# Transformer layer on one Trainium2 core: queries and keys by seven block products instead of eight, ahead of the attention loop

## What is computed

```
h = layernorm(x) * (1 + ca) + sa               # ca, sa, ga, ... are rows of silu(c) @ wmod, per batch
q = h @ Wq + bq ; k = h @ Wk + bk ; v = h @ Wv + bv          # (4, 512, 16 * 128)
w = softmax(q k^T / sqrt(128) + causal mask)   # per batch and head
x = x + ga * ((w v) @ Wo + bo)
h = layernorm(x) * (1 + cb) + sb
x = x + gb * (top-2 of 8 experts, SwiGLU, + a shared SwiGLU)(h)
```

## Time and profile before

| | us |
|---|---|
| three runs | 1672.33, 1673.3 (median), 1673.81 |
| the profiled execution's own time | 1676.7 |
| its span, first to last instruction | 1674.9 |
| TensorE busy (share) | 1591.5 (95%) |
| VectorE, ScalarE, GpSimd busy (share) | 891.5 (53%), 697.0 (42%), 591.2 (35%) |
| mean granted TensorE clock, share of full | 0.981 |

### The profile page before, as it was taken

The page is one execution under the profiler, slowest core; times in us unless marked ns, Lnnn a source line. Parts: engine busy times, 40 slices in busy tenths (PEclk is TensorE's granted clock), DMA queues, the critical chain, the costliest instruction groups (busy, mean ns, idle before and its releaser), DMA issues.

```text
span 1674.9 us, 29946 instructions
## 1 busy us (share of the span) xinstructions
PE 1591.5 (95%) x9012; PEld 1382.1 (83%) x9013; DVE 891.5 (53%) x2091; ACT 697.0 (42%) x1689; POOL 591.2 (35%) x625
## 2 busy tenths in 40 slices
PE   6999989999999999999999999978998899999997
PEld 3888578888888888888888888767898798888886
DVE  4333136666666566656665666767656322222267
ACT  4222155555555555555555555432231232222332
POOL 0001024544554535444545455655211211111043
PEclk9999999999999999999999999989998999999998
DMA  7522225243343253432423442585213445655455
GB/s 262 200 101 106 95 72 164 64 123 116 111 122 103 72 153 96 129 109 78 152 72 107 118 125 66 164 318 193 88 38 132 151 182 182 252 205 192 178 182 176
DMA packets 178453, 232.40 MB, mean 139 GB/s; under 512 B 78600, under 2 KB 137352, under 8 KB 175328
## 3 DMA queue, kind: packets, MB, share of 16 engines
q1 hardware_dynamic: 168112, 204.74, 37.0%
q0 software_dynamic: 5680, 18.62, 3.9%
q10 hardware_dynamic: 4608, 8.39, 1.6%
HBM read 151.70 MB, written 80.00 MB: 138 GB/s over the span
## 4 chain that ended last, share of the span: by engine, by line
PE 79%; DVE 8%; DMA 6%; ACT 3%; issue 3%; SPq 1%; another core or an unknown queue 0%; POOL 0%; ACTq 0%; DVEq 0%; POOLq 0%
PE bank L1118 48%; PE bank L1195 9%; PE bank L1279 7%; PE bank L1230 7%; DMA slot_results<-y_sb 5%; PE bank L1262 4%; PE bank L1131 1%; PE bank L1336 1%; PE bank L1362 1%; DVE o_lo L1604 1%; DVE pt_lo L1602 1%; ACT prob L939 1%; DVE ht_lo L1778 1%; DMA q_transposed<-q_out 1%; ACT o_hi L972 1%
## 5 line engine op out<-in xcount | busy, mean ns | idle before, releaser
L1118 PE MATMUL bank<-w,xt_hi 128*128 (+2 forms) x1136 | 287.0, 335 | 9.9 <-issue 8.2
L939 ACT ACTIVATE prob<-bank,neg_max 128x128 f32<-128x128 f32 (+3 forms) x256 | 134.0, 526 | 241.3 <-DVE neg_max L1643 238.7
L1118 PEld LDWEIGHTS bank<-w,xt_hi 128*128 128x128 f32 x1136 | 198.7, 191 | 22.0 <-issue 15.5
L680 POOL CAST q_hi<-q_raw 128x512 fp32r<-128x512 f32 x64 | 71.2, 1112 | 386.2 <-PE bank L1230 238.2
L1118 PE MATMUL bank<-w,xt_lo 128*128 (+2 forms) x568 | 185.6, 327 | 0.0
L1118 PE MATMUL bank<-w,ht_hi 128*128 (+3 forms) x426 | 142.6, 416 | 19.2 <-DVE ht_lo L1778 19.2
L1778 DVE TENSOR_TENSOR ht_lo<-bank,ht_hi 128x128 fp32r<-128x128 f32 (+1 forms) x213 | 48.4, 283 | 195.8 <-ACT ht_hi L1052 192.0
L1118 PE MATMUL bank<-wv_hi,h_lo 128*128 128x256 f32 x512 | 144.7, 283 | 0.0
L1118 PE MATMUL bank<-wv_lo,h_hi 128*128 128x256 f32 x512 | 144.5, 282 | 0.0
L1118 PE MATMUL bank<-wv_hi,h_hi 128*128 128x256 f32 x512 | 144.3, 282 | 0.0
L951 ACT ACTIVATE prob<-prob,row_inv 128x128 f32<-128x128 f32 (+3 forms) x256 | 136.2, 556 | 1.4
(11 more groups left out here) (203 smaller groups left out, 4081.6 us busy)
## 6 DMA issues: line engine op xcount, KB each, us to landing
ch_raw<-wexp SPq DMA_DIRECT2D x128, 170.0 KB, 2.6
experts_hi<-ch_hi SPq DMA_DIRECT2D x128, 170.0 KB, 2.0
experts_lo<-ch_lo SPq DMA_DIRECT2D x128, 170.0 KB, 2.1
w<-experts_hi SPq DMA_DIRECT2D x10, 2176.0 KB, 8.4
w<-experts_lo SPq DMA_DIRECT2D x10, 2176.0 KB, 15.0
q_transposed<-q_out SPq DMA_DIRECT2D x64, 256.0 KB, 2.0
q_raw<-q_transposed SPq DMA_DIRECT2D x32, 512.0 KB, 4.2
slot_results<-y_sb SPq DMA_DIRECT2D x39, 256.0 KB
```

Source lines behind the costliest of these rows:

```text
L680: pool.tensor_copy(hi, raw).then_inc(split_hi, 1)
L939: ins = act.activation(prob[:, h, ROW_AT[r]:ROW_AT[r] + (r + 1) * P], bank[2 + i % 2][:, at:at + (r + 1) * P], ACT.Exp, bias=neg_max[:, h, ...
L1118: ins = pe.matmul(dst, a, m, start=(k == 0), stop=(k == last))
```

## The change

Stage 1 now makes both queries and keys, all but the queries of the first two pairs by a scheme with seven block products in place of eight. A *unit* is a pair of heads of q or k, a *half* (`half(v)`) is a unit for two batches, taken as a 2 x 2 block matrix product: weights in blocks (two chunks of features) x (head), hidden state in blocks (batch) x (two chunks). 14 units, 28 halves. Each of the seven products is 2 chunks x 3 passes = 6 matmuls of 512 columns in a bank of its own, and the banks are taken in rotation over all eight. Four of the products take sums of weight blocks (made by GpSimd, `sums`), four take sums of blocks of the hidden state (`t_sums`). VectorE combines the seven banks to the four results in seven instructions; ScalarE copies the first bank out. Results of q are stored as before. Results of k are split there (hi on ScalarE, lo on VectorE once and GpSimd three times a half, through a ring of three buffers of 4 KB a partition) and stored to DRAM, 512 KB per result; the loop loads 1 MB of keys a step.

In the loop, the keys' products and their splitting are gone (and the splitting of wk on GpSimd), the probabilities have a buffer per head, and the orders of the queues are rearranged. At the end, the second `c_seed_of` on GpSimd comes after `c_pre(2)` instead of ahead of it.

The new tables and the head of TensorE's order:

```diff
+UNITS = [("q", 2), ("q", 3), ("k", 0), ("q", 4), ("k", 1), ("q", 5), ("k", 2), ("q", 6), ("k", 3), ("q", 7),
+         ("k", 4), ("k", 5), ("k", 6), ("k", 7)]
+HALVES = [(i, s) for i in range(NU - 2) for s in range(2)] + [(NU - 2, 0), (NU - 1, 0), (NU - 2, 1), (NU - 1, 1)]
+PREPARE = {1: 1, **{2 * i: i + 1 for i in range(1, NU - 1)}}
+MOD_AFTER = {4: 2, 8: 4, 12: 5}
+def stage1_order(plain, half):
+    plain(0)
+    plain(1)
+    half(0)
+    plain(2)
+    plain(3)
+    for v in range(1, NV):
+        half(v)
```

TensorE, stage 1 (`plain(b)`: q of the first two pairs for batch b, 48 matmuls; transposes of batch b+1 between):

```diff
+            def plain(b):
+                pe.wait_ge(hlo_ok, b * TT + TT)
...
+            def half(v):
...
+                def product(j, ws, ms):
+                    if free[j]:
+                        pe.wait_ge(*free[j])
+                    q = 0
+                    for (a_hi, a_lo), (m_hi, m_lo) in zip(ws, ms):
+                        for a, m in ((a_hi, m_hi), (a_hi, m_lo), (a_lo, m_hi)):
+                            ins = pe.matmul(bank[to[j]][:, :], a, m, start=q == 0, stop=q == 5)
...
+                product(0, plain_w(0, 0), rows(0))
+                product(1, sum_w(1), t_rows(2))
+                product(2, sum_w(2), t_rows(3))
+                product(3, sum_w(0), t_rows(1))
+                if v == 0:
+                    transposes(2, 0)
+                    transposes(2, 1)
+                product(4, plain_w(2, 0), rows(2))
+                if v == 0:
+                    transposes(2, 2)
+                    transposes(2, 3)
+                product(5, sum_w(3), rows(DC + 2))
+                product(6, plain_w(2, 1), t_rows(4))
```

VectorE and ScalarE, one half:

```diff
+                dve.tensor_tensor(g_s, p6, e1_s, ALU.add).then_inc(half_ok, 1)
+                dve.tensor_tensor(w_s, p7, g_s, ALU.add).then_inc(half_ok, 1)
+                if v in PREPARE:
+                    unit_low(PREPARE[v])
+                dve.tensor_tensor(u_s, p5, g_s, ALU.add).then_inc(half_ok, 1)
+                total(d22, p5, bb, w_s)
+                if v in PREPARE:
+                    sums_low(PREPARE[v])
+                total(d11, p2, ba, e1_s)
+                if kind == "k":
+                    dve.tensor_tensor(ring[n % 3][:, 1, :], g_s, ring[n % 3][:, 0, :].bitcast(F32),
+                                      ALU.subtract).then_inc(k22_ok, 1)
+                total(d12, p3, ba, u_s)
+                total(d21, p4, bb, w_s)
...
+                act.activation(e1_s, bank[half_banks(v)[0]][:, :], ACT.Copy).then_inc(e1_ok, 1)
+                if v in PREPARE:
+                    unit_high(PREPARE[v])
+                if kind == "k":
+                    for k, (done, src) in enumerate(((C22, g_s), (C11, e1_s), (C12, ct[0]), (C21, ct[1]))):
+                        n = 4 * K_NO[v] + k
+                        if n >= 3:
+                            act.wait_ge(k_st[n % 3], 16 * (n // 3))
...
+                        act.activation(ring[n % 3][:, 0, :], src, ACT.Copy).then_inc(kh_ok, 1)
```

A step of the loop on TensorE (before: see the lines above):

```diff
+                    values(0)
+                    values(1)
+                scores(2, n, here)
+                project(0)
+                project(1)
+                scores(3, n, here)
+                project(2)
+                scores(4, n, here)
+                project(3)
+                scores(5, n, here)
+                turn(0)
+                    values(2)
+                    values(3)
+                turn(1)
+                    scores(0, n + 1, there)
+                weigh(0)
+                    scores(1, n + 1, there)
+                weigh(1)
```

(the two queues are given here as lists; in the code they are calls in this order). In the first step ScalarE has `normalise(5); bias_rows(2); bias_rows(3)` ahead of `pt_part(1, 0)`, each `bias_rows` a copy of 128 x 2048. SP loads 1 MB of keys a step ahead (`load_k`). GpSimd: `split_q(1)` goes between the second and third weight chunk, `wk` is gone, and in the tail:

```diff
+                if tail == 1:
+                    c_seed_of(0)
+                if tail >= 0:
+                    c_pre(tail)
                 if last:
                     c_seed_of(1)
-                if tail >= 0:
-                    c_pre(tail)
```

More of the change, by code:

```diff
@@ L1591, in _ @@
-            with dve.Fori(1, B) as b:
-                batch(b)
-            for m in range(2, 6):
-                mod_piece(m)
+                h_low(0, i)
+            stats(1)
+            stats(2)
+            normalise(1)
+            hidden(1, 0)
+            hidden(1, 2)
+            for i in range(TT):
+                h_low(1, i)
+            t_sums(0)
+            unit_low(0)
+            sums_low(0)
+            t_low(0, (2, 3, 4))
+            normalise(2)
+            dve.wait_ge(const_ld, 5 * 16)
@@ L1597, in _, with plain @@
+            def plain(b):
+                if b == 2:
+                    hidden(3, 0)
+                    hidden(3, 2)
+                    for i in range(TT):
+                        h_low(3, i)
+                    t_sums(1)
+                    t_low(1, (2, 3, 4))
+                if b % 2:
+                    t_low(b // 2, (1,))
+            stage1_order(plain, half)
             stage1_over(dve)
```

1072 lines of the change are left out of this document (641 added, 431 removed).

## The result

The changed kernel took 1687.5 us (median of 4 runs, 1685.0 to 1689.2) against 1673.6 us of the kernel before on the same chip: ratio 1.0075, 95% interval 1.0058 to 1.0092. It is slower by 0.6 to 0.9%, where 0.9% faster was forecast. The profiled execution has a span of 1687.4 us, 12.5 more than before.

What follows compares the result with a forecast made beforehand. TensorE, busy 95% of the span, was taken as the bound. Handover +142.0, loop -141.4, tail -17.4 and seed +2.5 sum to -14.3 us, taken off the 1673.3 median: 1659.0 us, range 1637 to 1682.

Steps and rivals of the forecast that it cites:

- Part 1, the count: Matmuls for queries and keys: 1536 before, 1368 after; 168 fewer at 0.227 us each, 38.1 us.
- Part 2, stage 1: Query and key products start at 27.0 us and end at 365.8, with 7.0 us of new TensorE waits.
- the cover that I named: Key halves in stage 1: slow bank reads paid off by q halves in between, so lag costed at nothing.
- the third rival: Stage 1 key halves bound by splitting: 1678 us, chance 0.13; sign: waits on the stores of keys.
- Handover: Between stage 1 and loop: scores start at 377.2 us, first projection at 405.2, which is 142.0 later than before.
- the bare step: First attention step, run without projections: 28 us from the scores' start to the first projection.
- Part 3: Loop step: period falls from 27.375 to 22.5 us, 141.4 us back over 29 steps; keys' loads and GpSimd hidden.
- the wait of 0.9: Each loop step: TensorE idles 0.9 us ahead of `project(0)`, released by VectorE's `o_lo`.
- Part 4: Tail, step 30's projection to last output tile: 52.2 us instead of 69.6, 17.4 less.
- The second seed: Tail, GpSimd: seed after `c_pre(2)`, which waits for `xr`; costs 2.5 us, bounds 0 and 6.
- The one on the other side: Rival in the loop: longer chain, `o_part(1)` late on ScalarE, period from 23.0; at 23.3 1682 us; chance 0.17.
- TensorE stays the bound in the loop: Rival in the loop: period 21.7 us, total 1636 us, chance 0.17.

Runs made afterwards that it cites:

- 10: Changed kernel with the attention loop's two first loads issued behind the first store of the last half: 1692.8 us, ratio 1.0104 to the kernel before.
- 13: Kernel 9 plus 34 matmuls whose result nobody reads, ahead of the first scores: 1645.4 us, ratio 0.9822 to the kernel before.
- 9: Changed kernel with the three loop orders of 7 and both seeds put back as in 3: 1647.5 us, ratio 0.9852 to the kernel before.
- 6: Changed kernel with the next queries' load issued ahead of the next keys' load in every step: 1679.1 us, ratio 1.0028 to the kernel before.
- 7: Changed kernel with the orders of 5 and 6, and the value weights' split behind the third chunk: 1651.9 us, ratio 0.9863 to the kernel before.
- 5: Changed kernel with ScalarE's evacuation of head 1's output ahead of normalise(0) of the next step: 1691.3 us, ratio 1.0124 to the kernel before.
- 1: Changed kernel with the first seed put back behind the first expert chunk of step 30: 1684.6 us, ratio 1.0078 to the kernel before.
- 2: Kernel before with only the first seed moved late, behind all four expert chunks of step 30: 1683.7 us, ratio 1.0073 to the kernel before.
- 3: Changed kernel with both seeds of the last pair put back to their earlier places on GpSimd: 1682.4 us, ratio 1.0035 to the kernel before.
- 12: Kernel 9 plus reordered tail norm work and row-tile loads, with the first row tile's transposes behind the last output tiles: 1645.5 us, ratio 0.9829.
- 8: Changed kernel with the orders of 5 and 6, the value weights' split left behind the fourth chunk: 1657.0 us, ratio 0.9897 to the kernel before.

## Why the prediction was wrong

**Part 1, the count: right.** TensorE's busy time fell by 40.5 us for 38.1.

**Part 2, stage 1: right to the microsecond or so.** Products end at 366.7 (365.8), new waits 6.2 (7.0), and TensorE busy 268.00 of 268.00 us beside the key halves: the cover that I named held, and the third rival fell. Its sign did show, 36.2 us in 16 waits of ScalarE for the stores of keys, and TensorE felt none of it before the handover. The rule behind that rival shows elsewhere. Six instructions of the norm with both inputs in SBUF took 7.4 us (1105.5 to 1112.9) in the last stretch of the changed kernel, with GpSimd busy beside them; 6 x 0.75 are 4.5. The Trainium skill (SBUF — State Buffer, "Who interferes with whom") states that such an instruction contends with GpSimd's reads of SBUF, and the trace agrees, with 0.83 to 1.75 us for each of the six. `v_lo` and TensorE's wait of 4.98 us for it stand behind them, on the tail's path, where I had not looked for it.

**Handover: the landing of a store was mis-sized.** I took 3.2 us for 512 KB from a median of 2.0 for 256 KB; the median of all 64 such stores was 3.0, but with 1.5 MB of loads in front the one that mattered took 7.3, and the scores came at 381.6 for 377.2. The figure fits a store with nothing in front; what I left out was the queue. 10 took the loads away, and the wait for the buffer fell from 5.9 to 2.3 us. The other 2.0 us lie in the bare step (30.0 for 28.0); with TensorE kept busy in the gap (13) it was 28.3 for the 29.2 of 9, so some 0.9 of it can be the clock. The rest stays open.

**Part 3: the period was right, its cover was not.** 22.2 to 22.6 with 0.6 to 1.2 idle is what most ordinary steps show. The step that failed is the sentence "keys' loads ... and GpSimd ... are hidden by 17 us and 9 us". The keys' load was hidden; the queries' load behind it was not, and it heads GpSimd's chain of every step. I had asked whether the new transfer arrives in time and not what it delays. The mean was 22.70, 5.7 us over 29 steps; the seven changes of pair, 165.0 us for 157.5, hold more than all of it. 6 shows the cause of TensorE's waits there, the order of the two loads, though that order alone brought only 2.8 us of the loop back. 7 shows what it was worth with the rest: the wait of 0.9 could be taken out too, and the loop fell to 628 us. Without that order the same shortening lost time (5), partly by the clock.

**Part 4: the largest miss, 17.1 us.** Forecast 52.2, measured 69.3. In the table this term alone is more than the gain that was forecast. I costed the rows of the norm and the reordering on VectorE, but not the first `c_seed_of` that GpSimd's new order puts behind four chunks and a split: 11.7 us of the stretch by 1, and 12 us of the time of the kernel before by 2. In the changed kernel less of it reaches the end: both seeds put back give 7 us (3), and with the loop in order under 2, within the interval (9). So the seeds alone did not make the sign. With them back the kernel is still 0.35% slower than before, with the loads swapped 0.28%, and it is the loop's three orders together that turn it (7). The second seed, which I gave 2.5 with bounds 0 and 6, seems hidden as things were. What remained to 52.2 is the load of the row tile with the output tiles behind it; 12 took it out and reached 50.8, and the end did not follow. Had my stretch been right, part of its 17.4 us would probably have come back as a wait in stage 3, which my sum gave nothing.

**The rivals.** The one on the other side had the right sign and the wrong place: no period of 23 on ScalarE, but GpSimd's queue. "TensorE stays the bound in the loop" became true only in 7.

Left open: of all these orders only the seed was tried on the kernel before. The kernels at 0.982 to 0.985 therefore do not say what the seven products alone are worth, since other orders might make the kernel before faster too.

## What to carry to other kernels

When a step gets shorter, list for every engine what it does and in which order, the engines at 35% too: GpSimd had slack on average and was late at one instruction. For a new transfer, ask what stands behind it in its queue, and load first what heads a chain. Fixes of one chain must be tried together: an order that lost 0.5% alone (5) gained 1.3% beside another (8), and the seeds showed in the time only when both were put back.

## What the hardware showed

TensorE in the changed kernel behind its wait of 9.00 us:

```profile
381.50:402.00 20.50, 15.03 (x56) 12.53 (x57) 10.30 (x31) 17.75 (x35) 10.43 (x10) 0.58 0.51 171
```

A wait of TensorE can cost twice, and its length alone does not say whether it does. In the changed kernel the clock stayed at 1.00 in the 3.3 us behind a wait of 1.34 us; behind one of 2.31 us it fell 1.4 us later, to 0.57 in 570.5 to 573.0. In 5 it was 0.50 in the next 4 us behind waits of 3.61, 3.35 and 2.66 us, and 1.00 behind waits of 3.00 and 2.75. Behind the 9.00 us of the changed kernel it was 0.58 on average over 20 us, in which TensorE also had waits of its own. Work on nothing in the gap kept 1.00 there, and did not keep it behind, where the engine was again idle for a third of the time. The order of two loads in one queue moves time between them: 5.9 and 7.1 us with the keys first, 7.7 and 4.6 with the queries first. The Trainium skill (DMA: Bandwidth & Descriptors, "Two DMAs through the same engine are not ordered") says that descriptors of one queue on one DMA engine start in order, but that a later one may complete before an earlier one has finished writing. That each of the two loads lands sooner when it is issued first fits the first part; no trace here shows single descriptors, and none shows the second part.
